# Threshold search by quarters of the partitions, router moments from token rows, and a shorter last combination

## The reference, cut to what matters

```python
mod = (silu(c) @ wmod).reshape(8, 6, 1, -1)
sa, ca, ga, sb, cb, gb = (mod[:, i] for i in range(6))
ga = (2 * (ga >= 0) - 1) * max(abs(ga), 0.25)          # the same for gb
h = layernorm(x) * (1 + ca) + sa
x = x + ga * attention(h, W_qkv, W_o)
h = layernorm(x) * (1 + cb) + sb                        # "h2"
x = x + gb * ffn(h)
# ffn(h): router
mu, var = mean(h), var(h)
hn = (h - mu) * rsqrt(var + 1e-5) * ln_gamma + ln_beta
probs = softmax(hn @ Wr + br)                           # 8 experts
# each of W1, b1, W2, b2: k = 5% of its size; thr_top, thr_bot = k-th largest, k-th smallest |w|
# perturbed w = w - 0.8 w where |w| >= thr_top, w + 0.8 w where |w| <= thr_bot
y_e = gelu(h @ W1_e + b1_e) @ W2_e + b2_e
ffn = probs[0] * y_0 + sum(probs[1:]) * y_1
```

## Time and profile before

| | |
|---|---|
| median of three runs | 228.4 us |
| the profiled execution: its own time | 229.65 us |
| its span (first to last instruction) | 227.9 us |
| busy: PE / DVE / ACT / POOL | 208.2 / 174.3 / 163.6 / 131.0 us |
| granted TensorE clock, mean | 0.989 of 2.4 GHz |
| DMA | 19.84 MB, mean 87 GB/s |

### The profile page before, as it was taken

The page is one execution under the profiler, slowest core; times in us unless marked ns, Lnnn a source line. Parts: engine busy times, 40 slices in busy tenths (PEclk is TensorE's granted clock), DMA queues, the critical chain, the costliest instruction groups (busy, mean ns, idle before and its releaser), DMA issues.

```text
span 227.9 us, 5343 instructions
## 1 busy us (share of the span) xinstructions
PE 208.2 (91%) x1876; PEld 140.4 (62%) x1876; DVE 174.3 (76%) x534; ACT 163.6 (72%) x348; POOL 131.0 (57%) x211
## 2 busy tenths in 40 slices
PE   7686979999999999999998999998999979999993
PEld 3343646566576575666655666655677974786792
DVE  5675779998899899898889799769679493373465
ACT  2489678999999999999799799667759303344310
POOL 6852331765878867864764364379699826504600
PEclk9999999999999999999999999999999997999998
DMA  5848583984947046055238100000000010010011
GB/s 165 145 150 253 136 211 90 217 218 110 223 138 190 9 116 188 0 161 145 73 97 204 30 6 0 0 7 0 3 1 3 0 46 3 0 46 0 3 46 47
DMA packets 19350, 19.84 MB, mean 87 GB/s; under 512 B 1436, under 2 KB 17459, under 8 KB 18259
## 3 DMA queue, kind: packets, MB, share of 16 engines
q1 hardware_dynamic: 18778, 19.23, 32.2%
q10 hardware_dynamic: 544, 0.26, 0.4%
HBM read 14.11 MB, written 5.25 MB: 85 GB/s over the span
## 4 chain that ended last, share of the span: by engine, by line
PE 53%; ACT 15%; DVE 13%; issue 7%; DMA 6%; POOL 2%; SPq 2%; ACTq 0%; DVEq 0%
PE bank L923 11%; PE bank L903 10%; ACT msk L594 8%; PE bank L820 5%; ACT PT L578 4%; PE bank L799 3%; DMA Ks<-parts 3%; PE bank L777 3%; PE bank L886 2%; DMA wa<-in_w 2%; PE bank L773 2%; DVE nmax L1228 2%; PE bank L825 2%; PE bank L958 2%; PE bank L838 2%
## 5 line engine op out<-in xcount | busy, mean ns | idle before, releaser
L491 POOL TENSOR_SCALAR_AFFINE_SELECT PT<-PT 128x256 f32<-128x256 f32 (+1 forms) x96 | 47.6, 506 | 38.7 <-ACT PT L578 35.6
L594 ACT ACTIVATE msk<-wa,cand 128x1024 bf16<-128x1024 f32 (+1 forms) x62 | 60.4, 996 | 3.7 <-DVE cand L1214 3.6
L578 ACT ACTIVATE PT<-bank 128x512 f32<-128x512 f32 x96 | 55.1, 620 | 3.0 <-PE bank L794 2.2
L1228 DVE TENSOR_REDUCE nmax<-bank 128x2 f32<-128x512 f32 x64 | 43.6, 686 | 3.0 <-PE bank L777 2.3
L799 PE MATMUL bank<-Qs,Ks 80*128 80x256 bf16 x128 | 24.7, 274 | 1.8 <-ACT PT L578 1.3
L1224 DVE TENSOR_REDUCE nmax<-bank 128x4 f32<-128x512 f32 x32 | 21.7, 679 | 5.8 <-PE bank L770 5.8
L777 PE MATMUL bank<-Ks,Qs 78*128 78x256 bf16 x128 | 24.4, 272 | 0.0
L461 POOL TENSOR_TENSOR ex<-eul,lg 128x32 f32<-128x32 f32 x4 | 21.7, 5436 | 2.7 <-DVE lg L1283 2.7
L1316 DVE SCALAR_TENSOR_TENSOR yt<-bank,pr,yt 128x128 f32<-128x128 f32 x32 | 9.1, 345 | 17.2 <-PE bank L923 17.1
L820 PE MATMUL bank<-PT,Vx 128*32 128x256 f32 x256 | 20.4, 390 | 1.2 <-POOL PT L491 0.6
L773 PE MATMUL bank<-mask 128*128 128x256 bf16 x64 | 17.7, 276 | 2.9 <-DVE nmax L1228 2.1
(11 more groups left out here) (210 smaller groups left out, 468.3 us busy)
## 6 DMA issues: line engine op xcount, KB each, us to landing
Qs<-parts SPq DMA_DIRECT2D x7, 576.0 KB
Ks<-parts SPq DMA_DIRECT2D x7, 576.0 KB
parts<-part SPq DMA_DIRECT2D x7, 384.0 KB, 3.0
x_all<-in_x SPq DMA_DIRECT2D x8, 128.0 KB, 7.0
parts<-part SPq DMA_DIRECT2D x8, 128.0 KB, 2.9
rows_bc<-rows_out SPq DMA_DIRECT2D x2, 512.0 KB, 10.0
out<-ob SPq DMA_DIRECT2D x3, 256.0 KB, 2.3
wa<-in_w SPq DMA_DIRECT2D x2, 256.0 KB, 4.6
```

What stands on the lines that cost most here:

```text
L491: gp.affine_select(out=v, in_=v, compare_op=ALU.is_ge, fill=0.0, base=0, pattern=[[0, v.shape[1]], [1, P]], channel_multiplier=-1).then_in ...
L578: act.activation(PT[:, e % 2, j], psE[u % 2][:, :], ACT.Exp).then_inc(q["exp_done"], 1)
L594: act.activation(scratch, wa[:, 0:width], ACT.Sign, bias=cand[:, col:col + 1].bitcast(F32), scale=-(1.0 - 2.0 ** -24), accum_out=acc[:, co ...
L1228: ve.tensor_reduce(nmax[:, b % 2, 1, h:h + 2], bank.rearrange("p (h k) -> p h k", h=2), axis=AX.X, op=ALU.max, negate=True).then_inc(q["ma ...
```

## The change

**Search.** `wa` becomes 128 x 2048: a quarter of the partitions (32) holds a whole matrix, and each matrix is loaded twice (two DMAs of 512 KB where two of 256 KB were). There is one candidate per partition. ACT counts 1536 columns in one instruction (2048 in the `BY_ACT` bits), DVE still 512. The limits stand in a small tile. In the start, `first_parts` and `first_split` go ahead of the absolute values; DVE's absolute covers 1536 columns; `turned(1)` and `projected(1)` go ahead of the wait for the second part of the modulation weights, and `total(0)` behind it.

**Router moments.** The squares on DVE and the second set of matmuls go. Two modulation rows per batch are written to DRAM and broadcast back to all partitions (two DMAs of 512 KB, behind the last two stacks on SP). GpSimd multiplies and adds them on the token rows (`spread`, two operations of 128 x 512 per pair), DVE takes bn_stats and bn_aggr of four blocks (`third_stats`). `router_ln` for pairs 0 and 1 moves to steps 35 and 36; `router_logits(1)` to step 38. `second_normal(5)` moves behind `c_exp(0)`, the norms of batches 6 and 7 behind `c_exp(1)` and `spread(2)`. `c_pe_h(2)` moves ahead of `f2(1)`, `c_pe_h(3)` ahead of `f2(3)`.

**Last sums.** `combine(even)` also takes the gate and adds x; `combine(odd)` is then one fused operation a block (product with probability and gate row) and one addition. The last pair ends in three pieces: two blocks, one, one.

```diff
-            def sign_count(n, col, width):
+            def sign_count(n):
...
-                scratch = msk[:, 0:2].rearrange("p a f -> p (a f)") if col == TOP else b_scratch[:, 0:width]
+                width = 4 * FF if n in BY_ACT else ON_ACT        # ON_ACT = 3 * FF
-                    act.activation(scratch, wa[:, 0:width], ACT.Sign, bias=cand[:, col:col + 1].bitcast(F32),
-                                   scale=-(1.0 - 2.0 ** -24), accum_out=acc[:, col:col + 1])
+                    act.activation(scratch[:, 0:width], wa[:, 0:width], ACT.Sign, bias=cand[:, 0:1].bitcast(F32),
+                                   scale=-(1.0 - 2.0 ** -24), accum_out=acc[:, :])
...
             scaled(0)
+            first_parts()
+            value_copy(0)
             act.wait_ge(q["wa_in"], 32)
             act.activation(wa[:, 0:FF], wa[:, 0:FF], ACT.Abs).then_inc(q["wa_act"], 1)
-            first_parts()
+            scaled(1)
...
+            def spread(p, row):
+                ks = slice(4 * p, 4 * (p + 1))
+                bs = slice(2 * p, 2 * (p + 1))
+                if row == 2:
+                    gp.wait_ge(q["mod_in"], 16 * (p // 2 + 1))
+                    gp.wait_ge(q["h2T_psum"], p + 1)
+                else:
+                    gp.wait_ge(q["spread"], p + 1)
+                h2 = n2[:, ks, :].rearrange("p (b i) d -> p b i d", b=2)
+                gp.tensor_tensor(h2, h2, mod_bc[:, bs, row - 1, :].unsqueeze(2).broadcast_to([P, 2, NBLK, D]),
+                                 op=ALU.mult if row == 2 else ALU.add)
...
             if t == FFN_STEP:
                 c_exp(0)
-            second_rstd(B - 1)
-            second_normal(B - 1)
-            for p in range(1, NPAIR):
-                if p >= 2:
-                    router_ln(p)
-                c_exp(p)
+            second_normal(B - 3)
+            c_exp(1)
+            spread(2, 2)
+            spread(2, 1)
+            for b in (B - 2, B - 1):
+                second_rstd(b)
+                second_normal(b)
+            router_ln(2)
+            c_exp(2)
+            spread(3, 2)
+            spread(3, 1)
+            router_ln(3)
+            c_exp(3)
...
+            def third_stats(p):
+                v.wait_ge(q["h2_done"], p + 1)
+                for k in range(4 * p, 4 * (p + 1)):
+                    last = ve.bn_stats(st3[:, k, :], n2[:, k, :])
+                then_self(last)
+                for k in range(4 * p, 4 * (p + 1)):
+                    last = ve.bn_aggr(mv3[:, k, :], st3[:, k, :])
+                then_self(last)
+                ve.tensor_scalar(ve3[:, ks], mv3[:, ks, 1], EPS, None, op0=ALU.add)
+                ve.tensor_tensor(lt2[:, p % 2], e8(mv3[:, ks, 0]), g8(gsum[:, 0:NE]), op=ALU.mult)
...
             router_weights(0)
+            combine(0)
+            third_stats(2)
+            combine(1)
+            router_weights(1)
+            combine(2)
+            router_moments(2)
+            router_logits(2)
+            third_stats(3)
+            combine(3)
+            router_weights(2)
+            combine(4)
+            router_moments(3)
+            router_logits(3)
+            combine(5)
+            router_weights(3)
+            combine(6)
+            combine(7)
```

More of the change, by code:

```diff
@@ L451, in second_normal @@
                 last.then_inc(q["n2_done"], 1)
+            def spread(p, row):
[8 more added lines that the diff above has]
+                gp.tensor_tensor(h2, h2, mod_bc[:, bs, row - 1, :].unsqueeze(2).broadcast_to([P, 2, NBLK, D]),
+                                 op=ALU.mult if row == 2 else ALU.add).then_inc(q["spread" if row == 2 else "h2_done"], 1)
             def router_ln(p):
@@ L930, in total @@
                     return
-                if n not in BY_ACT:
-                    pe.wait_ge(q["m_dve"], sum(k not in BY_ACT for k in range(n + 1)))
                 if n == 0:
@@ L935, in total @@
                 claim_x((q["cand_done"], n + 2))
-                mm(psX[:, 0:2], halves[:, 1, :], (acc_z if n in BY_ACT else acc_d)[:, :], start=True, stop=False)
-                pe.wait_ge(q["m_act"], 2 * (n + 1))
-                mm(psX[:, 0:2], halves[:, 0, :], acc[:, :], start=False, stop=True).then_inc(q["tot_done"], 1)
+                if n not in BY_ACT:
+                    pe.wait_ge(q["m_dve"], sum(k not in BY_ACT for k in range(n + 1)))
+                    mm(psX[:, 0:1], quarters[:, 1, :], acc_d[:, :], start=True, stop=False)
+                pe.wait_ge(q["m_act"], n + 1)
+                mm(psX[:, 0:1], quarters[:, 0, :], acc[:, :], start=n in BY_ACT, stop=True).then_inc(q["tot_done"], 1)
             def turned(b):
@@ L1314, in combine @@
+                for k, (bank, blocks) in enumerate(LAST_PIECES if p == NPAIR - 1 else ((psU, range(4)),)):
                     v.wait_ge(q["f2_done"], n + 1 + k)
                     for i in blocks:
-                        last = ve.scalar_tensor_tensor(yt[:, w, i], bank[:, i * P:(i + 1) * P], pr[:, p % 2, w, i:i + 1],
-                                                       yt[:, 1 - w, i], op0=ALU.mult, op1=ALU.add)
+                        last = ve.scalar_tensor_tensor(yt[:, 1, i], bank[:, i * P:(i + 1) * P], pr[:, p % 2, 1, i:i + 1],
+                                                       rows_bc[:, 2 * p + i // NBLK, 1, :], op0=ALU.mult, op1=ALU.mult)
@@ L1478, in _ @@
                     perturb_b2()
-                if SQUARE_STEP <= t <= SQUARE_STEP + 1:
-                    squares(t - SQUARE_STEP)
             router_weights(0)
-            for n in range(2 * NPAIR):
-                combine(n)
-                p = n // 2 + 1
-                if p < NPAIR and n % 2 == 0:
-                    if p >= 2:
-                        router_moments(p)
-                    router_logits(p)
-                elif p < NPAIR:
-                    router_weights(p)
-                    if p + 1 < NPAIR:
-                        squares(p + 1)
+            combine(0)
[15 more added lines that the diff above has]
+            combine(7)
 def slopes():
```

257 lines of the change are left out of this document (125 added, 132 removed).

## The result

The changed kernel takes 248.57 us (median of 4 runs, 245.73 to 249.99), the kernel before 228.66 (4 runs beside them): a ratio of 1.0815, interval 1.0746 to 1.0884. The forecast was 222.9 with a range up to 227.0. The profiled execution took 245.73, with a span of 244.0 against 227.9, so 16.1 us are to be found in the two traces.

The account below looks back on a forecast made before the run. No one engine was taken to set the time: ScalarE is full mid-loop, nearly TensorE alone from step 33. Terms -2.0 + 0.8 - 4.3 = -5.5 us, from 228.4, gave 222.9 us, own range 220.9 to 225.2, 8 in 10 219.7 to 227.0.

Parts of the forecast that it names:

- Part 2: The start: `first_parts` no longer waits for `wa`, but 512 KB more are queued ahead; +0.8 us, ends -1.6 and +2.5.
- the end of +2.5: The start's upper end: the queue holds the write of the first parts back and the 8 KB rows move more slowly.
- the start costs more: Rival about the start: +2.5 us in place of +0.8, giving 224.6 us; chance 0.10.
- the term +0.8: The net forecast for the start: +0.8 us, with the first scores at about 19 rather than 18.1.
- Part 1: The search: one sign instruction a bit saves ScalarE 0.27 us; -2.0 us in all, ends 0 and -3.0.
- Part 3: Steps 24 to 39: second router matmuls go (-1.8), batch 5's norm leaves (-0.5), `third_stats(1)` costs +0.2; `f2(0)` 2.1 us earlier.
- Part 4: The feed-forward stage: a chain of GpSimd and VectorE ends at 221.4 rather than 225.6; -4.3 us.
- TensorE did not set the end: Rival about the last stage: TensorE still sets the end and the full gain comes through, 220.2 us; chance 0.13.
- the spreads were not dear: Rival about GpSimd's spreads: break-even at 2.55 us each; at 3.0 each +7.4, 230.3 us; chance 0.10.
- VectorE was not held by the power: Rival about the last stage: VectorE is held while GpSimd takes a power, +3.3, 226.2 us; chance 0.04.

Follow-up runs that it names:

- e1: The changed kernel with each copy of W1 and W2 loaded by its own plain DMA, four of 256 KB; 228.41 us, ratio 0.9947.
- e4: The kernel before with a second, unused copy of both weights, loaded by two more plain DMAs and waited for; 233.35 us, ratio 1.0143.
- e3: e1 with `third_stats(3)` moved from ahead of `combine(3)` to behind `router_weights(2)`; 224.55 us, ratio 0.9769.
- e5: The kernel before with each load of `wa` read as 2 x 32 interleaved rows, which can't be folded into one dimension; 240.66 us, ratio 1.0493.
- e15: The kernel before with each load of `wa` read as 4 x 16 interleaved rows; 235.19 us, ratio 1.0275.
- e6: The changed kernel with the first two source dimensions swapped: 32 rows first, then the zero-stride dimension of 2; 227.99 us, ratio 0.9896.
- e2: The kernel before with each load of `wa` written as two runs of 32 neighbouring rows; 230.55 us, ratio 1.0054.
- e7: The kernel before with only the search by quarters, its new start and four loads of 256 KB; 231.17 us, ratio 1.0025.
- e12: The same kernel as e3, measured once more; 224.52 us, ratio 0.9814.
- e14: e3 with the last sums of the kernel before; 224.61 us, ratio 0.9769.
- e11: e3 with the search, the loads and the start of the kernel before; 224.05 us, ratio 0.9806.
- e13: e11 with the last sums of the kernel before, leaving the new router moments with a late `third_stats(3)`; 224.06 us, ratio 0.9743.
- e9: The kernel before with only the last sums in their new form; 233.05 us, ratio 1.0144.
- e10: The changed kernel with 76 spare matmuls on TensorE in the wait for `wa`; 246.79 us, ratio 1.0720.

## Why the prediction was wrong

**The step that failed is the price of the load in Part 2**: "512 KB more are in the queue ahead of everything else. The DMA engines move 230 GB/s there ... so they empty 2.2 us later". It counted bytes at the rate of all the engines. e1 and e4 show that count to be right for plain loads (+2.2 to +2.9 us until `wa` is used, in e3 +3.3). But the two DMAs of the change have a source of `[[0, 2], [4 * FF, QUART], [1, 4 * FF]]`, an outer dimension of 2, and ran on about 2 engines of 16: `wa` landed 19.3 us later (28.2 for 8.9), and the addition for batch 0 came 20.5 us later, where +0.8 was forecast. I had looked at the size of the DMA and not at its pattern. e5 (2, by stride) and e15 (4) show that the outer dimension is what counts, e6 that the zero stride is not. Neither the end of +2.5 nor the rival "the start costs more" covered this case, as both were bounds on the same rate. The Trainium skill says as much (DMA: Bandwidth & Descriptors, Why a DMA increments its semaphore by 16 and not by 1): a DMA is dealt to the largest number of engines, up to 16, that divides the slowest dimension larger than 1 on both sides. By that rule it is 2 for the change, 4 for e15 and 16 for e6, and the shares of 0.13 and 0.27 agree; that e2 kept its speed fits it if the pattern that counts is the folded one.

**Moving `first_parts` ahead of `wa`** (a gain of up to 1.6 us in Part 2) came to nothing in after: `scaled(1)` stands behind the absolute of `wa` on ScalarE, TensorE's `projected(1)` waits for it (the L976 at 29.36), and the scores stand behind that. Part 2 had missed this second way from `wa` to the scores. With plain loads it went as Part 2 had it, a little worse: the first write of the parts is issued at 9.7 in e3 and e7 (forecast 9.6) and at 10.5 in e1, for 11.2 before, but lands at 14.8 in e1, 15.0 in e3 and 15.2 in e7 (forecast 14.1), for 13.3 before; the first products of the scores come 1.1 us later in e1 (19.44 for 18.36), where 0.9 was forecast. With plain loads the term +0.8 measured +0.7 to +2.2 at batch 0 (e3, e1, e12, e7, e14), its upper half.

**Part 1** was near: -2.0 forecast for the search, -1.7 measured from batch 0 to batch 7 (e7 against before), and 1.5 to 1.6 where e3, e12 and e14 are set against e11 and e13; the bits ahead of batch 0 can't be told from the rest of the start. One reading in it was wrong: in the earlier trace rows TensorE with 15.55 and not VectorE with 15.36 is the next bound behind ScalarE's 16.11, and the 0.95 are what TensorE lacks to 16.50. The 1.56 us of a sign with its read was the trace's to 0.01.

**Part 3** was too large: -2.1 forecast, -1.0 to -1.1 measured (e11 and e13 against before, 104.7 and 104.8 for 105.8). `f2(0)` begins at 187.65; with the start and the search taken off (some 20.5 - 1.8 = 18.7) that is 168.95, where 168.3 was forecast.

**Part 4** had the right chain. With the same 18.7 taken off, the chain reads: `c_exp(0)` 165.0 (forecast 164.2), `c_exp(1)` 173.4 (171.35), the spreads of pair 2 done at 181.9 (179.3), `c_exp(2)` 191.9 (189.6), `c_exp(3)` 209.9 (207.9), the end 223.2 (221.4). So it starts 0.8 late; then it loses 1.0 in a wait that I had missed: `c_exp(1)` writes the tile that `router_weights(0)` reads, and waits for it (the 1.01 in GpSimd's timeline). The remaining differences are 0.8 us at the end of the spreads of pair 2 (of which 0.45 is the longer power, 5.89 us, and 0.2 the spreads of 1.27 for 1.16) and nothing at the end. The two parts come to -2.4 (223.2 for 225.6), not -4.3. And what the tail gives of it is no more than the clock's: from batch 7 to the end e15, with the tail of before at a clock of 1.00, takes 55.5, and after 55.4. That the new sums shorten nothing by themselves was right inside the change, and too kind to them alone (e9).

**The rivals.** TensorE did not set the end, the spreads were not dear (1.27 against the 2.55 at which the change breaks even), and VectorE was not held by the power: in after its operations with two inputs in SBUF took their usual 0.69 us at 193.37 and 196.06, inside the power that began at 192.10. The hold of this rival is real all the same, for a spread in place of a power (e3, 1.6 us).

Gain was lost in two places: the search gives 1.7 and its start takes it; the tail gives 1.7 in after and 4.5 in e3, because `third_stats(3)` stood two functions too early. The prediction had put that in bold and priced it, but not asked what moving it would bring.

## What to carry to other kernels

Price a DMA by its pattern first and by its bytes second: with an outer dimension of 2 half a megabyte ran at 51 to 54 GB/s and one megabyte at 54 to 55, where plain rows ran in a queue that moved 230. On an engine that works in order, put the instruction that waits longest behind all the work that does not need it: here that alone took 2.8 us off the tail (52.6 for 55.4). Keep VectorE's operations with two inputs in SBUF clear of GpSimd's large ones, and look for such an operation that takes longer than its like. An edit that is free inside one version can cost 1.4% in another; take each part alone before it is called neutral.

## What the runs showed that I had not expected

- Behind the slow load the queue that issues was slow too: 5.55 us for the issue of a 2 KB vector at 7.37, against 0.36 before, and 7.09 in e10; with half the bytes (e5) no issue took over 2.09.
- Keeping TensorE busy in a long wait kept its clock at 1.00 and did not keep it up afterwards: it fell behind 3.47 us of idleness, and was at 0.50 from 33 to 46 us.
- GpSimd's power took 5.88 to 5.89 us for `c_exp(1)` and 5.43 for the other three in all kernels with the new moments; VectorE runs `router_weights(0)` and `combine(0)` beside it there, but that this is the cause is not shown.
